# Second attention: the first expert's rows scaled by ScalarE and added by GpSimd from the fourth sequence on

## What is computed

```python
top_w, top_idx = jax.lax.top_k(logits, TOP_K)          # TOP_K = 2
top_w = jax.nn.softmax(top_w.astype(jnp.float32), axis=-1)
combine = jnp.zeros((t, e), x.dtype).at[jnp.arange(t)[:, None], top_idx].add(top_w)
...
out = jnp.einsum('ted,te->td', y, combine)
...
x = x + _L0_ffn_ref(_layernorm(x, axis=-1), ...)
x = x + _L1_attn_ref(_layernorm(x, axis=-1), ...)
```

## Time and profile before

| | before |
|---|---|
| median of 3 runs | 2822.84 us (2822.49 to 2823.51) |
| profiled execution, its own time | 2810.92 us |
| span of that execution in the trace | 2808.9 us |
| busy, share of the span: TensorE / its weight load / VectorE / ScalarE / GpSimd | 87% / 77% / 65% / 48% / 29% |
| VectorE busy in 1420 to 1645 us (three turns of 75 us) | 189.2 us of 225 |
| TensorE, ScalarE, GpSimd busy there | 178.4, 89.5, 144.6 us |

### The profile page before, as it was taken

The page is one execution under the profiler, slowest core; times in us unless marked ns, Lnnn a source line. Parts: engine busy times, 40 slices in busy tenths (PEclk is TensorE's granted clock), DMA queues, the critical chain, the costliest instruction groups (busy, mean ns, idle before and its releaser), DMA issues. The chain is left out here.

```text
span 2808.9 us, 53468 instructions
## 1 busy us (share of the span) xinstructions
PE 2444.4 (87%) x20412; PEld 2173.2 (77%) x20412; DVE 1828.7 (65%) x3234; ACT 1343.2 (48%) x2053; POOL 814.7 (29%) x1194
## 2 busy tenths in 40 slices
PE   4999999952899999745777888869999999999999
PEld 3666666631899999624666777769999999999999
DVE  7666666663688888679888878457454454544544
ACT  1555555620577777432334443434554545545454
POOL 4556666237000000145666655510000000000000
PEclk7999999975899999867899999989999999999999
DMA  9994000003677777556555455235222222232222
GB/s 300 330 329 152 2 2 2 2 29 124 201 234 231 240 230 236 166 155 155 130 144 134 133 130 139 59 121 158 93 80 97 85 91 85 80 97 86 91 78 87
DMA packets 194350, 373.31 MB, mean 133 GB/s; under 512 B 28708, under 2 KB 104680, under 8 KB 193128
## 3 DMA queue, kind: packets, MB, share of 16 engines
q1 hardware_dynamic: 184792, 343.31, 40.5%
q0 software_dynamic: 9360, 27.27, 2.8%
HBM read 336.95 MB, written 100.66 MB: 156 GB/s over the span
## 5 line engine op out<-in xcount | busy, mean ns | idle before, releaser
L2300 DVE TENSOR_TENSOR e_h_lo<-e_h,e_h_hi 128x512 fp32r<-128x512 f32 x320 | 222.1, 694 | 300.7 <-ACT e_h_hi L2376 300.7
L2438 PE MATMUL e_h_ps<-e_yT_hi,e_w_hi 128*128 128x256 f32 x1280 | 362.5, 283 | 3.0 <-ACT e_h L2362 2.2
L2454 PE MATMUL e_y_ps<-e_w_hi,e_h_hi 128*128 128x256 f32 x1280 | 358.9, 280 | 2.3 <-DVE e_h_lo L2300 2.2
L2438 PE MATMUL e_h_ps<-e_yT_lo,e_w_hi 128*128 128x256 f32 x1280 | 358.4, 280 | 0.0
L2438 PE MATMUL e_h_ps<-e_yT_hi,e_w_lo 128*128 128x256 f32 x1280 | 358.3, 280 | 0.0
L2454 PE MATMUL e_y_ps<-e_w_hi,e_h_lo 128*128 128x256 f32 x1280 | 355.4, 278 | 0.0
L2454 PE MATMUL e_y_ps<-e_w_lo,e_h_hi 128*128 128x256 f32 x1280 | 355.3, 278 | 0.0
L2376 ACT ACTIVATE e_h_hi<-e_h 128x512 fp32r<-128x512 f32 x320 | 202.2, 632 | 277.2 <-DVE e_h L2295 220.9
L2362 ACT ACTIVATE e_h<-e_h_ps,e_b 128x512 f32<-128x512 f32 x320 | 218.8, 684 | 174.9 <-PE e_h_ps L2438 152.6
L2295 DVE TENSOR_TENSOR e_h<-e_h,e_spread 128x512 f32<-128x512 f32 x256 | 176.9, 691 | 133.3 <-ACT e_h L2362 132.2
L462 DVE TENSOR_REDUCE a_top<-a_ring 128x2 f32<-128x1024 f32 (+3 forms) x256 | 204.2, 819 | 71.5 <-PE a_ring L651 70.0
(11 more groups left out here) (364 smaller groups left out, 6835.8 us busy)
## 6 DMA issues: line engine op xcount, KB each, us to landing
e_w<-in_w SPq DMA_DIRECT2D x78, 1024.0 KB, 5.8
e_spread<-share_store SPq DMA_DIRECT2D x512, 128.0 KB, 2.9
a_keys<-rows_store SPq DMA_DIRECT2D x128, 256.0 KB, 4.9
a_queries<-rows_store SPq DMA_DIRECT2D x86, 256.0 KB, 5.0
a_running_hidden<-rows_store SPq DMA_DIRECT2D x42, 256.0 KB, 4.9
e_xs<-sorted_x SPq DMA_DIRECT2D x39, 256.0 KB, 5.0
sorted_y<-e_ys POOLq DMA_DIRECT2D x39, 256.0 KB, 6.0
e_stage_buf<-in_w_all SPq DMA_DIRECT2D x10, 512.0 KB, 4.2
```

The source lines that it names most:

```text
L2300: dve.tensor_tensor(h_parts[q % 2][1][:, :], h[:, q % 2, :], h_parts[q % 2][0][:, :], ALU.subtract).then_inc(h_lo.sem, h_lo.tick())
L2438: last = pe.matmul(h_ps[q % 2][:, cols], l, r, start=(m == 0), stop=(m == len(ops) - 1))
L2454: last = pe.matmul(y_ps[n][:, 0:D], h_parts[q % 2][a][:, n * P:(n + 1) * P], w2[b][:, c, :], start=(q == 0 and m == 0), stop=(q == CH - 1 ...
```

## The change

From the fourth sequence on (s >= 3, that is in turns 0 to 4), ScalarE multiplies the rows in `zn` by the first share in place (`scale_first`, after the denominator in stage 5 for LEFT, before the normalisation in stage 6 for RIGHT), GpSimd adds them to `x` (`add_first`, in stages 6 and 7 between its sum of the heads and the low part of the hidden values), and VectorE's `combine` does only the second expert's, waiting for GpSimd's add instead of the fetch. `combined` is counted in twos there, so that its counts stay as they were.

```diff
+        first_scaled, first_added = sig("first_scaled", TB), sig("first_added", TB)
...
+            def add_first(s, tiles):
+                for n in tiles:
+                    pool.wait_ge(first_scaled.sem, first_scaled.at(n + 1, s - 3))
+                    pool.tensor_tensor(g.x[:, s * TB + n, :], g.x[:, s * TB + n, :], zn[:, n, :],
+                                       ALU.add).then_inc(first_added.sem, 1)
...
+                if c in (6, 7) and live(s + 3):
+                    add_first(s + 3, range(2 * (c - 6), 2 * (c - 5)))
...
             def combine(s, tiles):
                 first = 2 * tiles[0]
-                for k in range(2):
+                for k in range(2) if s < 3 else (1,):
                     for i, n in enumerate(tiles):
-                        if k == 0:
+                        if s >= 3:
+                            dve.wait_ge(first_added.sem, first_added.at(n + 1, s - 3))
+                        elif k == 0:
                             dve.wait_ge(gathered[n].sem, 32 * (s + 1))
                         else:
                             dve.wait_ge(combined.sem, combined.at(first + i + 1, s))
...
+            def scale_first(s, tiles):
+                for n in tiles:
+                    act.wait_ge(gathered[n].sem, 32 * (s + 1))
+                    act.activation(zn[:, n, :], zn[:, n, :], ACT.Copy, scale=token(g.share[0], s, n)).then_inc(first_scaled.sem, 1)
...
+                if c in (5, 6) and live(s + 3):
+                    scale_first(s + 3, range(2 * (c - 5), 2 * (c - 4)))
```

More of the change, by code:

```diff
@@ L1586, in combine @@
                         dve.scalar_tensor_tensor(out=g.x[:, s * TB + n, :], in0=got(n, k), scalar=token(g.share[k], s, n),
-                                                 in1=g.x[:, s * TB + n, :], op0=ALU.mult, op1=ALU.add).then_inc(combined.sem)
+                                                 in1=g.x[:, s * TB + n, :], op0=ALU.mult,
+                                                 op1=ALU.add).then_inc(combined.sem, 1 if s < 3 else 2)
                 for i, n in enumerate(tiles):
-                    dve.wait_ge(combined.sem, combined.at(first + len(tiles) + i + 1, s))
+                    dve.wait_ge(combined.sem, combined.at(first + (len(tiles) + i + 1 if s < 3 else 2 * i + 2), s))
                     dve.bn_stats(stats[:, s % 2 * TB + n, :], g.x[:, s * TB + n, :]).then_inc(stat_step.sem)
```

## The result

The changed kernel takes 2844.24 us, median of 5 runs (2840.55 to 2851.77), the kernel before 2822.84 beside it (2821.31 to 2826.7): ratio 1.0077, 95% interval 1.0058 to 1.0096. That is 21 us slower, where 4.4 were forecast and the range ended at 2833.

The account below looks back on a forecast made before the run. VectorE, without idle time around the second attention's combines, was taken to move the turn one for one. Losses of 4.0 us in turns 1 to 4 and 0.4 in turn 0, added to 2822.8, gave 2827.2 us; range 2815 to 2833.

Parts of the forecast that it names:

- ScalarE, on the path nothing.: Stages 5 and 6: 20 added scalings of 0.5 us each fit ScalarE's idle time and cost nothing on the path.
- GpSimd, an add 0.70, the two of stage 6 done at +3.5.: Turn 2, counted from the end of the denominator's last product: adds of 0.70 us, the second done at +3.5.
- The wait of some 3.0, the last fetch back near 1 us.: Stage 6, turns 1 to 4: VectorE idles some 3 us for GpSimd's add; stage 5's last fetch falls from 2.68.
- "VectorE's first combine comes at +2.9, beside the second add, and ends at +3.8.": Stage 6, turn 2: first combine collides with one add, second ends at +5.2, stage 7 starts +5.8; 3.6 us lost.
- Stage 7.: Second pair comes at +10.7, both combines collide, stage 0 begins at +13.55 against +11.49; 1.5 of 3.6 us comes back.
- Stage 0 to mix without a collision, 11.94.: VectorE and GpSimd's low parts miss each other, so mix begins at +25.5 in turns 1 to 4; 4.0 us lost together.
- Turn 0, a loss of 0.4, at most 1.1.: No wait; 0.8 a stage saved, but the heads' later low part collides; bounds 1.5 us gain to 1.1 loss.
- Rival: TensorE's clock.: Longer idling before stage 1's value products lowers TensorE's clock: 1.27 us a turn, 5.1 in all, 2832.3 us; chance 0.30.
- Rival: VectorE gets in first, 2815.5.: Stages 6 and 7: VectorE's combines start before GpSimd's low parts, no collisions, 7.3 us saved; chance 0.14.

Follow-up runs that it names:

- vector_adds: Changed kernel, but VectorE adds the rows that ScalarE scaled, with a plain add, and GpSimd adds nothing: 2813.61 us, ratio 0.9964 to the kernel before.
- spare_scale: Kernel before, with ScalarE's 20 scalings added at their places and written into a spare tile that nobody reads: ratio 0.9973 to the kernel before.
- The kernel with the gap: Changed kernel, but GpSimd, after its two adds of stage 6, waits until VectorE has combined those tiles: 2824.56 us, ratio 1.0003 to the kernel before.
- late_low: Kernel before, but in stage 7 of turns 1 to 4 GpSimd's low part of the hidden values waits for VectorE's second-pair combines: 2807.51 us, ratio 0.9976.
- wait_both: Changed kernel, but VectorE waits for both GpSimd adds of a pair before its first combine of that pair: 2840.58 us, ratio 1.0084 to the kernel before.
- split_low: Changed kernel, but GpSimd computes the low parts of hidden values and heads in stage 6 in two 128x256 halves each: ratio 1.0032 to the kernel before.
- right_only: Change applied to tiles 2 and 3 only, tiles 0 and 1 combined as in the kernel before: 2820.5 us, ratio 1.0019 to the kernel before.
- left_only: Change applied to tiles 0 and 1 only, tiles 2 and 3 combined as in the kernel before: ratio 1.0118 to the kernel before.
- wide_add: Changed kernel, but GpSimd adds both tiles of a pair in one 128x512 instruction and VectorE waits for it: 2854.55 us, ratio 1.0128 to the kernel before.
- prefix: Changed kernel, but VectorE copies one element a partition between its wait and the first combine of stage 6: 2847.3 us, ratio 1.0084 to the kernel before.

## Why the prediction was wrong

A small loss was forecast and a loss came, and the sizes of the new work were right. One step failed that carries nearly all of the miss: a collision was priced at one instruction of GpSimd's.

- *ScalarE, on the path nothing.* Right. 20 scalings at 494 ns each; vector_adds and spare_scale have them and are faster than before.
- *GpSimd, an add 0.70, the two of stage 6 done at +3.5.* Right: 0.73 and 0.72, done at +3.49. The rule of the Trainium skill (GPSIMD Engine Reference, 4.1 Engine selection) holds too: GpSimd's adds step by 0.68, VectorE's in vector_adds by 0.33. But being twice as dear is not what was lost.
- *The wait of some 3.0, the last fetch back near 1 us.* Right: 2.92 and 1.09. The kernel with the gap, which keeps this wait and loses the hold, costs 4.6 in the stretch, near the 4.4 of the prediction, and has mix at +25.2 to +25.9 in turns 1 to 4, where +25.5 was forecast. There is luck in this: stage 0 begins at +12.9 there and not at +13.55, from it to mix it is 12.3 to 13.0 and not 11.94, and by the medians of the runs the loss is only 1.4.
- *"VectorE's first combine comes at +2.9, beside the second add, and ends at +3.8."* **This step failed.** It came at +2.92 and ended at +7.55. Stage 7 began at +9.0 in place of +5.8. I had drawn the rule "ends about 0.28 after GpSimd's instruction" from rows where VectorE and GpSimd took turns, and applied it to a combine that comes into a run already under way. GpSimd's three instructions went on at 1.26 to 1.27 each.
- *Stage 7.* Nearly right in its length, 7.4 from the start of stage 7 to that of stage 0, forecast 7.75; but only the second combine of the pair collided (1.51), the first was free (0.48), where both were to collide.
- *Stage 0 to mix without a collision, 11.94.* Wrong by 1.2 in turn 2: L1615 still took 1.13. Mix began at +29.5 in place of +25.5, and so in turns 3 and 4; +30.5 in turn 1. Set beside the earlier trace rows, mix comes 5.9, 4.5, 5.7 and 5.0 later after the product in turns 1 to 4, where 0.9, 0.5, 1.7 and 0.9 were forecast. Some of it is made good between a mix and the next product, so from one mix to the next it is 5.1, 4.5, 5.2 and 3.7, 18.5 together, against the forecast 4.0.
- *Turn 0, a loss of 0.4, at most 1.1.* Failed by the same step: its product lost 4.4, over five instructions of GpSimd's. I had counted collisions of one instruction only.
- *Rival: TensorE's clock.* It did not come as priced, 5.1 on the waited path. The six products for values ahead of mix in turns 1 to 4 (stage 1 of turns 2 to 5 by the count of the earlier trace rows), after (table by stretches):

```profile
1397.90:1400.20 2.30, 1.70 (x6) 0.83 0.22 72
1476.80:1478.95 2.15, 2.04 (x6) 0.76 0.19 65
1555.70:1558.15 2.45, 2.35 (x6) 0.65 0.25 84
1634.60:1637.40 2.80, 2.70 (x6) 0.56 0.31 104
```

  The same four took 2.23, 1.66, 2.93 and 2.93 before (the second and the last are the earlier trace rows): 9.75 together, and 8.79 now. But the twelve output products right behind them lost more than that, 10.12 together after 7.57. Those of turn 2, before and after:

```profile
1454.06:1455.66 1.60, 1.60 (x12) 1.00 0.78 214
```

```profile
1478.67:1481.44 2.77, 2.76 (x12) 0.52 0.82 226
```

  So the granted clock did fall more here, from 1.00 to 0.52 in this group, and TensorE's two groups are 1.6 us longer over the four turns. It is not on the path: these products end at 1481.44, mix begins at 1482.07, and VectorE has no idle time before it. From mix to the next product the change takes 49.4 in turns 1 to 3, where before took 49.4, 49.9 and 50.6.
- *Rival: VectorE gets in first, 2815.5.* In stage 7 of the change it does for one combine of the two; in stage 6, where the loss is, it does not. In late_low and spare_scale, where VectorE does come first in stage 7, the gain in the stretch is 6 to 7 us.
- The Trainium skill (SBUF — State Buffer, Who interferes with whom) calls the shared port pair an exclusive lock and says, of VectorE's 2-port modes, that whoever issues first gets it for the whole instruction; its Summary: rules for kernel authors says the same of a VectorE instruction with two SBUF inputs beside a GpSimd one that reads SBUF. Here the second one waited for more than the instruction that it met: for up to six of GpSimd's in a row. A range built on one instruction per collision was too narrow by this. The gap kernel shows the hold to be the cause; that the port pair is what VectorE waits for is the skill's account of it, which no run here tests by itself, and why it waits for more than one instruction stays open.

## What to carry to other kernels

Work moved to GpSimd can cost more than its own time when VectorE has instructions with two SBUF inputs, as it did here (23.5 us in the stretch, for 20 adds of which GpSimd was busy 16 us, on an engine that had idle time): look at how long GpSimd's run without a pause becomes, and at which instruction of VectorE comes into it. If VectorE must come in, try a wait of GpSimd's for it right there: one such wait took 18.9 us off the stretch of the change, and one 7.3 off that of the kernel before. And test each half of a change alone: here the first half was slower than the whole (1.0118 against 1.0077), and the second cost far less (1.0019).

## What the runs showed of the hardware

- A two-input instruction of VectorE can be held out by a run of GpSimd's: 4.63, 3.94, 7.58, 4.61, 7.00 us for an instruction of 0.47, and up to 5.26 for one of 0.68.
- GpSimd's own of 128x512 are not slowed meanwhile (1.25 to 1.29). Where the engines take turns, both are: combines at 1.5 and L1538 at 1.46, halves at 0.98 and 0.90.
- A small instruction of VectorE with one input can be delayed as well: the one of 128x8 in the variance took 1.13 in turn 2, beside L1547 of the change and L1538 of the kernel before, and 0.17 in turn 3 of the kernel before.
- When VectorE is let in stays open. In stage 6 of turns 1 to 4 of the change, of wait_both and of split_low it got in beside an instruction of 128x256, in right_only, left_only and wide_add only at the run's end. Against a rule by width: turn 0 of the change and of split_low has narrow instructions that did not let it in, and in stage 7 of before it got in behind one of 128x512. The product of turn 0 came 0.54 us after the start of the heads' low part in the change and 0.51 after it in prefix, and took 5.10 and 2.62. Whether it follows on its own instruction (prefix) or how much of GpSimd's is left (wait_both) did not decide it.
